# Linear-attention projections and the second bias in 16-bit parts, and every instruction given a new place

## The reference

```python
# 1 linear attention, 16 heads of 8 channels
q = gelu(x @ Wq.T + bq) + 0.21;  k = gelu(x @ Wk.T + bk) + 0.21;  v = x @ Wv.T + bv
z = 1 / (q . mean(k) + 1e-6)                      # per head and token
kv = rope(k).T @ v * scale**2;  out = (rope(q) @ kv) * z
block = layernorm(out + x) * gamma + beta
# 2 cross attention, 16 heads, on a context of 77 tokens
block = softmax((x @ Wq + bq) (ctx @ Wk + bk).T / sqrt(8)) (ctx @ Wv + bv) @ Wo + bo
# 3 mixture of 16 experts (128 -> 256 -> 128), each token's best 4 by a softmax router
block = sum_e c[token, e] * (gelu(x @ w1[e] + b1[e]) @ w2[e] + b2[e])
```

## Time and profile before

| | |
|---|---|
| median of 3 runs (lowest, highest) | 672.42 us (671.56, 672.63) |
| the profiled execution: its own time, its span | 671.28 us, 669.5 us |
| mean granted clock of PE | 0.934 |
| busy share of the span: PE, PEld | 89%, 66% |
| DVE, ACT, POOL | 63%, 63%, 36% |

### The profile page before, as it was taken

The page is one execution under the profiler, slowest core; times in us unless marked ns, Lnnn a source line. Parts: engine busy times, 40 slices in busy tenths (PEclk is TensorE's granted clock), DMA queues, the critical chain, the costliest instruction groups (busy, mean ns, idle before and its releaser), DMA issues.

```text
span 669.5 us, 16331 instructions
## 1 busy us (share of the span) xinstructions
PE 597.3 (89%) x6356; PEld 439.3 (66%) x6356; DVE 419.7 (63%) x1435; ACT 424.4 (63%) x532; POOL 241.4 (36%) x162
## 2 busy tenths in 40 slices
PE   3635868979999999999999999999999999899993
PEld 2613754658776776777776877677776766586673
DVE  1354576636785678766885778577866785266444
ACT  2521726776558765795569755985598558955660
POOL 4540431433325422553225422643244332342331
PEclk9555679989999999999999999999998999999999
DMA  7340011000100021002100110002000100000000
GB/s 198 108 107 23 18 38 45 4 17 18 34 18 2 2 66 34 4 2 57 42 3 2 50 35 19 2 17 61 23 4 2 33 25 5 1 18 1 1 17 17
DMA packets 30309, 19.67 MB, mean 29 GB/s; under 512 B 4616, under 2 KB 28920, under 8 KB 30232
## 3 DMA queue, kind: packets, MB, share of 16 engines
q1 hardware_dynamic: 22664, 13.20, 7.2%
q10 hardware_dynamic: 7280, 5.01, 2.5%
q0 software_dynamic: 288, 0.42, 0.3%
HBM read 8.85 MB, written 2.10 MB: 16 GB/s over the span
## 4 chain that ended last, share of the span: by engine, by line
PE 67%; ACT 13%; issue 7%; DVE 4%; SPq 1%; ACTq 1%; DMA 0%; POOL 0%; POOLq 0%; DVEq 0%
PE ps L934 15%; PE ps L910 8%; PE ps L912 7%; PE ps L911 7%; PE ps L871 5%; ACT g L655 4%; PE ps L930 3%; ACT w_stage L618 3%; PE ps L932 3%; PE ps L931 3%; ACT L618 2%; ACT L655 2%; PE ps L724 2%; PE ps L834 2%; PE ps L779 1%
## 5 line engine op out<-in xcount | busy, mean ns | idle before, releaser
L478 POOL TENSOR_TENSOR gl<-g,gh 128x1024 f16<-128x1024 f32 x64 | 136.7, 2136 | 236.8 <-ACT gh L644 236.3
L655 ACT ACTIVATE g<-ps,b 128x512 f32<-128x512 f32 x256 | 167.7, 687 | 61.0 <-PE ps L912 59.5
L1237 DVE SCALAR_TENSOR_TENSOR acc<-ps,cw,acc 128x128 f32<-128x128 f32 x448 | 126.0, 344 | 107.0 <-PE ps L934 65.0
L934 PEld LDWEIGHTS ps<-w,g 128*128 128x128 f32 x1024 | 121.2, 192 | 15.7 <-issue 11.6
L934 PE MATMUL ps<-w,g 128*128 128x128 f32 x1024 | 127.5, 278 | 2.2 <-DVE acc L1237 2.0
L910 PE MATMUL ps<-x2h,w1h 128*128 128x512 f16 x256 | 98.9, 387 | 7.0 <-ACT g L655 6.0
L912 PE MATMUL ps<-x2h,w1l 128*128 128x512 f16 x256 | 98.5, 385 | 0.0
L911 PE MATMUL ps<-x2l,w1h 128*128 128x512 f16 x256 | 98.5, 385 | 0.0
L930 PE MATMUL ps<-w2h,gh 128*128 128x128 f16 x512 | 89.3, 219 | 1.7 <-DVE acc L1237 1.5
L932 PE MATMUL ps<-w2h,gl 128*128 128x128 f16 x512 | 89.0, 219 | 0.0
L931 PE MATMUL ps<-w2l,gh 128*128 128x128 f16 x512 | 89.0, 219 | 0.0
(11 more groups left out here) (161 smaller groups left out, 876.7 us busy)
## 6 DMA issues: line engine op xcount, KB each, us to landing
q_rep<-qx SPq DMA_DIRECT2D x90, 32.0 KB
x<-in_x SPq DMA_DIRECT2D x8, 256.0 KB, 3.3
w_stage<-in_L_ffn_w ACTq DMA_DIRECT2D x1, 2048.0 KB, 18.4
q_swap<-q SPq DMA_DIRECT2D x16, 128.0 KB, 2.1
out<-fin SPq DMA_DIRECT2D x8, 256.0 KB, 2.4
k_rep<-kx SPq DMA_DIRECT2D x96, 19.2 KB
cx<-in_ctx SPq DMA_DIRECT2D x8, 154.0 KB
w<-in_L_ffn_w ACTq DMA_DIRECT2D x2, 512.0 KB, 4.8
```

Source lines behind the costliest of these rows:

```text
L478: pool.tensor_tensor(gl[:, j % SPLIT_RING, :, :], g32[:, e % RING, :, :], gh[:, j % SPLIT_RING, :, :], ALU.subtract).then_inc(s["lo"], 1)
L655: act.activation(g32[:, e % RING, h, :], bH[:, h, :], ACT.Gelu, bias=b1[:, e, h:h + 1], scale=1.0 / WS).then_inc(s["gelu"], 1)
L934: m = pe.matmul(o, g32[:, e % RING, h, tok], w2[:, j, h, :], start=(h == 0), stop=(h == HALF - 1))
L1237: m = dve.scalar_tensor_tensor(out=(acc_all if e == E - 1 else acc)[:, b, :], in0=bY[:, b * P:(b + 1) * P], scalar=cw[:, b, e:e + 1], in1= ...
```

## The change

1. q, k and v of the linear attention: weights and x are held as a high and a low float16 part. The high part is rounded (ACT), the low one is the difference (DVE, `xl`, a new step). Each float32 product becomes three float16 products: high x high, high x low, low x high. The weights are scaled by 256 (`WS`), and ACT and DVE take the factor out with the bias.
2. b2: DVE writes c into `cw_hl` as three 16-wide pieces (high, low, high; the new step `cw_hl`), one float16 transpose for each sequence brings them into 48 rows, and `b2_hl` holds (high, high, low). One float16 product over 48 rows then gives all three terms.
3. All tables of places are new, those of the filling and of the weight loads too.

```diff
-PE_AT = dict(x_t=1, q=4, kv01=6, kv23=9, k_mean=13, kv=28, den=33, out=33, cx_t=42, v1=44, x1_t=50, k=45,
-             q_x=60, scores=(8, 8, 10, 12, 12, 14, 15, 16), max_t=17, scores_t=(24, 28, 34, 40), values=(36, 37,
+PE_AT = dict(x_t=3, q=10, kv01=12, kv23=17, k_mean=22, kv=28, den=29, out=36, cx_t=43, v1=47, x1_t=54, k=52,
+             q_x=63, scores=(8, 8, 9, 10, 10, 12, 13, 14), max_t=19, scores_t=(24, 30, 38, 40), values=(37, 40,
...
-            pool.dma_start(b2[:, :], A["L0_ffn_b2"]).then_inc(s["i_b2"], 16)
+            for i in range(3):
+                pool.dma_start(b2[i * E:(i + 1) * E, :], A["L0_ffn_b2"]).then_inc(s["i_b2"], 16)
...
-                    act.copy(x_t[:, :], bE).then_inc(s["x_tc"], 1)
+                    act.copy(xh[:, :], bE).then_inc(s["xh"], 1)
...
-                    pe.matmul(bE, wq_t[:, :], x_t[:, :], start=True, stop=True).then_inc(s["q_p"], 1)
+                    pe.matmul(bE, wqh[:, :], xh[:, :], start=True, stop=False)
+                    pe.matmul(bE, wql[:, :], xh[:, :], start=False, stop=False)
+                    pe.matmul(bE, wqh[:, :], xl[:, :], start=False, stop=True).then_inc(s["q_p"], 1)
...
-                            m = pe.matmul(bE[:, b * 2 * P:(b + 1) * 2 * P], x_t[:, (2 * j + b) * P:(2 * j + b + 1) * P],
-                                          wkv_t[:, :, :], start=True, stop=True)
+                            pe.matmul(o, xh[:, tok], wkvh[:, :, :], start=True, stop=False)
+                            pe.matmul(o, xh[:, tok], wkvl[:, :, :], start=False, stop=False)
+                            m = pe.matmul(o, xl[:, tok], wkvh[:, :, :], start=False, stop=True)
...
-                        m = pe.transpose(ps[0:E, 4, b * P:(b + 1) * P], cw[:, b, :], ident)
+                        m = pe.transpose(ps[:, 4, b * P // 2:(b + 1) * P // 2].bitcast(F16), cw_hl[:, b, :, :], ident16[:, :])
...
-                        m = pe.matmul(bE[:, b * P:(b + 1) * P], cw_t[:, b * P:(b + 1) * P], b2[:, :], start=True, stop=True)
+                        m = pe.matmul(bE[:, b * P:(b + 1) * P], cw_t[:, b * P:(b + 1) * P], b2_hl[:, :], start=True, stop=True)
...
+                if p == at["xl"]:
+                    since(dve, "xh", a + 1)
+                    dve.tensor_tensor(xl[:, :], bE, xh[:, :], ALU.subtract).then_inc(s["xl"], 1)
...
+                    for part in (0, 2):
+                        dve.tensor_scalar(cw_hl[:, :, part, :], cw[:, :, :], WS * WS, None, ALU.mult).then_inc(s["cwh"], 1)
+                    since(dve, "cwh", 2 * (f + 1))
+                    dve.scalar_tensor_tensor(out=cw_hl[:, :, 1, :], in0=cw[:, :, :], scalar=WS * WS, in1=cw_hl[:, :, 0, :],
+                                             op0=ALU.mult, op1=ALU.subtract).then_inc(s["cwl"], 1)
```

More of the change, by code:

```diff
@@ L89 @@
[L89 to L126, removed]
+PE_AT = dict(x_t=3, q=10, kv01=12, kv23=17, k_mean=22, kv=28, den=29, out=36, cx_t=43, v1=47, x1_t=54, k=52,
+             q_x=63, scores=(8, 8, 9, 10, 10, 12, 13, 14), max_t=19, scores_t=(24, 30, 38, 40), values=(37, 40,
+             42, 43), wo=50, x2_t=63, logits=0, c_t=58, b2=63, first=3, next=0, second=0, u_t=(42, 44), ao_t=48)
@@ new lines @@
+ACT_AT = dict(x_t=5, q=10, kv23=22, cx_t=46, x1_t=60, k=52, q_x=63, max_t=17, scores_t=(28, 37, 39, 40),
+              x2_t=63, weights=0, c_t=63, gelu=1, high=3, u=(40, 43), ao_t=49)
+DVE_AT = dict(q=17, kv01=11, kv23=18, k_rot=23, k_mean=23, kv=27, den=31, out=35, norm1=39, norm2=44, x1=45,
+              v1=46, k=53, q_x=63, scores=(7, 7, 7, 8, 9, 11, 15, 15), max=16, pairs=(42, 44), wo=51, x2=60,
+              x2_t=62, logits=0, weights=2, cw=10, b2=61, combine=0, finish=44, q_sin=29, sums=18, xl=7,
+              cw_hl=41)
@@ new lines @@
+POOL_AT = dict(x_beta=25, k_rot=21, q_rot=31, res=34, norm1=37, norm2=48, x1=32, x2=56, finish=36, low=2)
+PE_FIRST = dict(x_t=6, q=7, kv01=28, cx_t=0, kv23=30, v1=48, k=55, k_mean=46, kv=51, den=58, out=60, x1_t=63,
+                q_x=63)
+PE_EARLY = dict(scores=(0, 0, 0, 1, 1, 1, 1, 3), max_t=6, scores_t=(15, 24, 26, 33), values=(25, 32, 37, 52),
+                u_t=(49, 55), ao_t=57, wo=57, x2_t=63)
+PE_ONE = dict(x_t=0, q=4, kv01=7, kv23=9, k_mean=20, kv=26, den=33, out=36, cx_t=51, v1=55, k=57, x1_t=60,
+              q_x=61)
@@ new lines @@
+PE_ZERO = dict(x_t=0, q=1, kv01=3, kv23=9, k_mean=22, kv=25, den=26, out=28, cx_t=39, v1=46, x1_t=63, k=55,
+               q_x=63, scores=(3, 5, 6, 8, 8, 14, 14, 17), max_t=21, scores_t=(25, 27, 28, 34), values=(29, 31,
+               37, 39), wo=62, x2_t=63, logits=0, c_t=57, b2=60, first=2, next=0, second=2, u_t=(39, 48),
+               ao_t=51)
+ACT_FIRST = dict(x_t=5, q=9, cx_t=16, kv23=19, k=37, x1_t=63, q_x=63)
+ACT_EARLY = dict(max_t=2, scores_t=(16, 17, 28, 38), u=(38, 43), ao_t=54, x2_t=63)
@@ new lines @@
+DVE_ONE = dict(q=14, kv01=6, kv23=17, k_rot=18, k_mean=17, q_sin=29, kv=31, den=31, out=39, norm1=40, v1=42,
+               norm2=50, k=55, x1=60, q_x=64, xl=1)
+DVE_ZERO = dict(q=13, kv01=3, kv23=10, k_rot=20, k_mean=19, kv=23, den=24, out=27, norm1=31, norm2=37, x1=53,
+                v1=48, k=54, q_x=63, scores=(3, 3, 6, 8, 9, 13, 16, 16), max=17, pairs=(40, 47), wo=60, x2=62,
+                x2_t=63, logits=2, weights=3, cw=13, b2=58, combine=1, finish=50, q_sin=19, sums=7, xl=0,
+                cw_hl=25)
@@ L566, in linear @@
                     since(act, "q", a)
[L567 removed]
+                    act.activation(qg[:, :], bE, ACT.Gelu, bias=bq[:, :], scale=1.0 / WS).then_inc(s["qg"], 1)
                 if p == at["kv23"]:
```

81 lines of the change are left out of this document (59 added, 22 removed).

## The result

| | before | after |
|---|---|---|
| median of the runs (lowest to highest) | 672.52 us (671.56 to 672.83, 4 runs) | 651.01 us (649.39 to 651.70, 4 runs) |
| profiled execution: time, span, mean clock | 671.28, 669.5, 0.934 | 651.37, 648.6, 0.948 |
| start of the router of body 0 | 103.78 | 99.68 |
| body 0 | 75.23 | 72.15 |
| bodies 1 to 5 together | 359.75 | 346.98 |

The ratio is 0.968, 95% interval 0.966 to 0.970: 21.5 us less, where 16.7 were forecast. A body is taken here from the start of its router to that of the next; the differences of the five rows add up to the 20.9 us between the spans. Of a kernel's executions the medians here hold all, and the ratios leave out those that took over 1.5% more than its fastest.

A forecast was written before the change was run, and what follows sets the result against it. PE was taken to set the pace, busy 70.0 of a full body's 71.3 us. The terms, -12.0 - 3.7 - 6.5 + 3.9 + 1.6 = -16.7 us, took 671.28 to 654.6, median 655.7; forecast 648 to 662 (0.54), range 644 to 665.

The forecast's parts named there:

- A: PE's time in the bodies: 16-bit products save 0.64 us for q, k, v and 1.02 for the bias, 12.0 in all.
- B: The filling: earlier first scores and transposed scores and cheaper k and v, -3.7 us, between -6 and -1.
- C: Two fewer table loads on ACT in each of bodies 1 to 6: -6.5 us, between -1 and -9.6.
- rival 2: The new order is better than read: q_rep in time, hidden waits go too; -27.6 us, 644.8; chance 0.20.
- D: New wait of PE's scores for q_rep in bodies 1 to 6, 1.3 us each, half counted: +3.9 us.
- E: End of body 0: the late output projection makes PE wait for x2n, +1.6 us, between 0 and +3.
- Rival 3: Slower: q's spread starts late behind k's, PE stands over 3.4 us in bodies 1 to 6; 678.8 us; chance 0.06.
- Rival 4: 16-bit products don't pay: k and v cost as 512 columns each, about 663.5 us; chance 0.18 shared with another rival.

The follow-up runs named there:

- run 2: The kernel before with the changed kernel's places, its float32 products kept: 662.44 us, ratio 0.979.
- run 3: The changed kernel with q, k and v back in float32, only the bias in 16-bit parts: 662.13 us, ratio 0.985.
- Run 4: The changed kernel with the old places in the filling, in body 0 and for the weight loads: 657.71 us, ratio 0.977.
- run 9: The changed kernel with a single-column unused exponential at place 35 of bodies 1 to 7, one more pair of table loads: 658.51 us, ratio 0.983.
- run 7: The changed kernel with the next group's query projection earlier, at places 60 (PE, ACT) and 61 (DVE) instead of 63: 658.39 us, ratio 0.978.
- run 11: As run 7, with ACT's copy of the router's transposed weights also moved from place 63 to 61: 650.22 us, ratio 0.969.
- run 12: The edits of run 10 and run 11 together, and DVE's part of the query projection at 59: 647.94 us, ratio 0.967.
- run 8: The changed kernel with body 0's output projection back at place 57 (PE 62, DVE 60 in the changed kernel): 650.74 us, ratio 0.970.
- run 1: The kernel before with the new 16-bit products for q, k, v and the bias in the old places: 664.22 us, ratio 0.988.
- Run 6: The changed kernel with the second transposed-scores exponential at place 32 instead of 37, making three groups: 681.74 us, ratio 1.016.
- run 5: The changed kernel again with no edit, as the measure for later runs: 655.13 us, ratio 0.972.
- run 10: The changed kernel with POOL's x_beta of the filling's second group waiting for DVE's x1 of the first: 649.74 us, ratio 0.967.

## Why the prediction was right, and where not

The sum came out near the measured time, but partly because its misses have both signs. By stage, in us from the profile (the forecast from the terms as they stand, 16.7 in all; measured 20.9 between the spans):

| | forecast | measured |
|---|---|---|
| filling and body 0 | -3.8 | -7.2 |
| bodies 1 to 5 | -9.0 | -12.8 |
| body 6 | -2.9 | -1.4 |
| body 7 | -1.0 | +0.4 |

**A, PE's time: right in kind, 14% too large.** I had 0.64 + 1.02 = 1.66 us a body; by PE's busy time in runs 2, 3 and after it is 0.54 + 0.89 = 1.43. k and v came as priced (12 products in 1.30). q is 0.76 and not 0.65, because its first product shows 0.32 and not 0.22, and so is the bias, 0.32 from its start to the next step:

```profile
378.00 0.40 PE L913 MATMUL ps<-b_hl,cw_t 48*128 48x128 f16 x4
378.32 0.23 PE L945 MATMUL ps<-w2h,gh 128*128 128x128 f16 x1
```

I had set aside 0.06 us for a change of shape; these two places alone lose 0.2. And the bias doesn't pay in all eight bodies: in body 7 PE is busy for 0.7 us less, but waits for the gelu (0.7) and for `cw_t` (0.5) that before hadn't, and the body is no shorter. The Trainium skill's 81 ns for a sustained 128-column product ("TensorE: Matmul & The Clock Gate", "Back-to-back issue gap") isn't borne out: the four transposes of c take 0.22 us, 55 ns each, though the bias by itself, at the change of shape, has 80.

**B, the filling: 3.7 forecast, 4.1 measured to the router of body 0, and the nearness is luck.** The first scores came 3.4 us earlier and not 0.95. My base, an input ready at 54.6, was wrong: x1, which I left where it was, ended 1.9 us earlier (42.07 against 44.01), 1.1 by its start and 0.8 by its length. The first transposed scores came 5.7 us earlier, at 64.02. Behind them 4.0 us were lost again by the start of x2n, for which I had no term (95.99 against 97.68 in the earlier trace rows):

```profile
95.99 1.11 DVE L1181 TENSOR_SCALAR x2n<-y,mv,rstd 128x128 f32<-128x128 f32 x4 [1.12 <-POOL rstd L438]
```

And of the 4.1 us about 1.5 are q's place behind the router, as said above. Run 4 doesn't measure B alone, because of its wait for `xl`. The order that POOL and a DMA happen to take moves x1 between 1.11 and 3.98 us (runs 2 and 9 at the ends), and the moment at which the clock rises moves the rest.

**C, the table loads: the mechanism right, the size too small in bodies 1 to 5.** The exponential has 16 loads where it had 22, as forecast. I took 0.8 us a body of a pair. Run 9 gives 1.35 for a pair put back. Run 2, where all places change alone, has a body 1.28 shorter than the undisturbed 71.33; that is the new order as a whole, and no run takes the loads alone out of before. That PE waits only 1.1 us a body was no bound: its idle time fell from 1.3 to 0.6, and its busy time by 0.57 as well (70.02 to 69.45), with the same instructions. What in PE's rows became shorter wasn't followed; it is what rival 2 called hidden waits under the 70.0 us. In body 6 the ACT waits fell by 2.1 us (2.5 forecast), but other waits took most of it (`q_rep` 0.8, mx 0.6 more, acc 0.4): 1.4 us in all. The Trainium skill's 2.66 us for a change of table ("ScalarE: Activation LUTs", "What ACT_TABLE_LOAD costs") would make run 9's pair 5.3 us of ACT; the trace has 2.7.

**D, the wait for `q_rep`: right.** Forecast 1.3 us of standing, half of it counted; measured 1.0 us a body, and run 3 shows that it gives back about 0.7 of the bias's gain. It isn't the bound for itself: runs 7, 11 and 12 took it away in all but one or two of bodies 1 to 6 and found `cw_t`, `x2l` and `x2n` right behind. At the end of a body several chains through ACT, DVE and SP end within about 1 us of each other.

**E, the end of body 0: not borne out.** Forecast +1.6. The wait for x2n is there, 0.9 us, but run 8 shows the late place (62) to be 0.8 us better than 57, since it spares PE the wait for acc. Against place 54 of before it wasn't measured.

**What no term held: the clock inside the bodies.** In these two profiles it makes an estimated 4.6 us, more than the 4.2 that I was short between the spans. In before, after a wait of 0.50 us at 214 and one of 0.59 at 216.15, the granted clock fell (PE's row, then us, busy, clock, DMA share, GB/s):

```profile
216.15 0.61 PE L910 MATMUL ps<-x2h,w1h 128*128 128x512 f16 x1 [0.59 <-ACT g L655]
```

```profile
216.00:217.00 1.00, 0.85 (x3) 0.58 0.00 0
...
218.00:219.00 1.00, 1.00 (x7) 0.50 0.09 16
219.00:220.00 1.00, 1.00 (x32) 0.71 0.00 0
```

The same happened at 503, and at 137.7 behind a wait of 1.70. Bodies 1 and 5 of before take 72.93 and 72.85 us, the three between them 71.33: some 1.55 us for each such fall, and the estimate takes the same for body 0. After has none past 104 us. The rows were in my reach (bodies 1 and 5 stood out in the trace of before), and I took 71.3 for all. So 12.8 us in bodies 1 to 5 are 5 x 1.43 (A) + 5 x 1.28 (the new order, C in it) - 5 x 0.8 (D, the growth of PE's idle time from run 2 to after) + 3.1 (two falls) = 12.7. That the change takes such falls away for good isn't shown: run 4 has the same places in bodies 1 to 5 and had one, behind the very wait that D names.

Rival 3 (q's spread late behind k's) didn't come: in the body from 440 us on, the issues for k and the zeros end at 447.8 and the copy of q, which the spread needs, at 448.2, so the wait was 1.0 us and not 3.4. Rival 2 was right about the hidden waits and wrong about `q_rep`. Rival 4 is excluded by the rows of k and v.

## What to carry to other kernels

Price a removed wait by a run that puts it back, not by the wait that PE shows: PE's idle time was 1.3 us a body, and the new places won 1.28 with 0.6 us of idle time still there (run 2). Where several engines' chains end together at the end of a loop body, an edit to one of them buys only the distance to the next; here three edits in a row bought nothing in bodies 1 to 5 and 1.0 us in body 6. Compare equal bodies with each other before summing: one that stands out by 1.5 us shows a cost that isn't in any instruction. And check a clock column against the duration of a product that you know at both levels.

## What the runs showed of the hardware

- The clock falls inside a body of nearly full PE work. In before and run 1, whose bodies have waits of 0.50 and 0.59 us 2 us apart, it fell in 3 of 10 bodies, each time to 0.5 for about 3.4 us. Run 6, with a wait of about 3.1 us in its bodies, had it in three of five. Run 4 had it once in five, behind a wait of 1.69 us. In after and runs 2, 3, 5, 7, 8, 9, 10, 11 and 12, bodies 1 to 5 had none, with single waits up to 1.5 us. What decides between the 3 and the 7 of 10 stays open.
- In the filling the clock rises at a different moment from execution to execution, with the same program up to there: at 79.9 and 88.0 us in the two profiles of the changed kernel, at 75.8 in run 8. In the same two profiles a fall inside body 0 adds 2.5 us in one. These are the profiled parts of the new kernel's spread, 647 to 658 us over ten executions; the other eight have no profile.
- DVE's operations on float32 tiles in SBUF nearly stand still while POOL works on its own: the four of x1 took 1.11 us with none of `x_beta` and `w1l` beside them (run 10), 2.10 with 1.4 us of these (the changed kernel) and 3.88 with 3.4 us (run 5).
